# Attention row sums spread by VectorE and DMA instead of TensorE, longer PV runs, one PV bank for two query groups

## The reference, cut to what matters

```python
mod = (_silu(L0_c) @ L0_wmod).reshape(1, 6, 1, -1)           # sa, ca, ga, sb, cb, gb
h = _layernorm(x) * (1 + ca) + sa
qkv = jnp.einsum('bse,ehd->bshd', h, w_qkv)                  # E=128, H=16, 3*64
q, k, v = jnp.split(qkv, 3, axis=-1)
logits = where(tril, einsum('bqhd,bkhd->bhqk', q, k) / sqrt(64), very_low)
att = einsum('bhqk,bkhd->bqhd', softmax(logits), v)
x = x + ga * einsum('bshd,hde->bse', att, w_out)             # ga, gb kept off zero
h = _layernorm(x) * (1 + cb) + sb
expert = argmax(h @ Wr.T + br)                               # 8 experts
y = W2[expert] @ relu(W1[expert] @ h + b1[expert]) + b2[expert]   # 128 -> 512 -> 128
x = x + gb * y
```

## Time and profile before

| | |
|---|---|
| time, median of 3 | 1067.04 us (1066.79 to 1068.41) |
| profiled execution, its own time | 1067.29 us |
| its span, first to last instruction | 1065.5 us |
| mean granted clock of TensorE | 0.98 |
| TensorE busy | 999.7 us (94%) |
| ScalarE busy | 718.6 us (67%) |
| VectorE busy | 701.0 us (66%) |
| attention's steady part | 38 to 948 us |
| routing and scatter | 948 to 1000 us |
| 23 expert tiles | 1000 to 1064 us |

### The profile page before, as it was taken

How to read it: one execution, slowest core, us unless ns; L and a number is a source line. 1 busy time by engine, 2 the same in 40 slices (tenths; PEclk the granted TensorE clock), 3 DMA queues, 4 the chain that set the end, 5 groups by cost and what they waited for, 6 DMA issues and landing times.

```text
span 1065.5 us, 19784 instructions
## 1 busy us (share of the span) xinstructions
PE 999.7 (94%) x7275; PEld 762.3 (72%) x7275; DVE 701.0 (66%) x2234; ACT 718.6 (67%) x1317; POOL 43.1 (4%) x55
## 2 busy tenths in 40 slices
PE   4999999999999999999999999999999999986386
PEld 2677777777777777777777777777777777755376
DVE  4976667856866577666785686657766678555264
ACT  2977767767667677776776776767777677642264
POOL 0000000000000000000000000000000000002444
PEclk9999999999999999999999999999999999996699
DMA  9300020002100020002000210002000100030210
GB/s 202 70 21 1 22 50 21 2 10 48 34 1 2 20 51 21 1 21 50 22 1 19 47 26 1 2 20 51 21 2 21 41 21 1 2 99 16 59 50 17
DMA packets 33199, 31.53 MB, mean 30 GB/s; under 512 B 12181, under 2 KB 22209, under 8 KB 33104
## 3 DMA queue, kind: packets, MB, share of 16 engines
q1 hardware_dynamic: 31856, 28.15, 11.3%
q0 software_dynamic: 1248, 2.13, 0.6%
HBM read 9.83 MB, written 4.12 MB: 13 GB/s over the span
## 4 chain that ended last, share of the span: by engine, by line
PE 85%; DVE 5%; issue 3%; POOL 2%; ACT 1%; DMA 1%; DVEq 1%; SPq 0%; POOLq 0%
PE ps L619 25%; PE ps L656 24%; PE ps L630 22%; PE ps L598 5%; PE ps L639 3%; PE ps L667 3%; PE ps L602 2%; POOL x_sorted L557 1%; DVEq L1067 1%; DVE q_split L926 1%; ACT q_split L791 1%; PE ps L707 1%; PE ps L733 1%; DVE accT L1086 1%; DVE v_sb L1100 1%
## 5 line engine op out<-in xcount | busy, mean ns | idle before, releaser
L619 PE MATMUL ps<-k_split,q_split 128*128 128x512 f32 (+2 forms) x1280 | 370.1, 396 | 4.1 <-DVE q_split L926 2.0
L805 ACT ACTIVATE probs<-probs,neg_max 128x128 f32<-128x128 f32 (+15 forms) x256 | 308.5, 1206 | 41.7 <-DVE neg_max L954 39.4
L947 DVE TENSOR_SCALAR_CACHE_REDUCE probs<-ps 128x512 f32<-128x512 f32 (+1 forms) x384 | 249.6, 667 | 100.0 <-PE ps L630 66.7
L813 ACT COPY pT<-ps 128x512 f32<-128x512 f32 (+1 forms) x435 | 234.2, 564 | 109.7 <-PE ps L630 105.6
L630 PE MATMUL ps<-ident,probs 128*128 128x128 f32 x2176 | 304.4, 273 | 1.4 <-DVE pT L966 1.3
L630 PEld LDWEIGHTS ps<-ident,probs 128*128 128x128 f32 x2176 | 256.0, 140 | 60.7 <-issue 29.4
L656 PE MATMUL ps<-pT,v_sb 128*64 128x256 f32 (+1 forms) x2304 | 272.6, 373 | 0.0
L619 PEld LDWEIGHTS ps<-k_split,q_split 128*128 128x128 f32 x1280 | 201.0, 190 | 48.8 <-issue 28.6
L656 PEld LDWEIGHTS ps<-pT,v_sb 128*64 128x64 f32 x2304 | 152.3, 136 | 87.1 <-issue 26.6
L950 DVE CUSTOM_DVE_ANT_0 probs<-ps,causal 128x256 f32<-128x256 f32 (+3 forms) x256 | 130.9, 511 | 27.6 <-PE ps L619 26.3
L966 DVE COPY pT<-ps 128x512 f32<-128x512 f32 (+1 forms) x141 | 92.3, 659 | 32.9 <-PE ps L630 30.2
(11 more groups left out here) (126 smaller groups left out, 610.4 us busy)
## 6 DMA issues: line engine op xcount, KB each, us to landing
k_split<-k_split SPq DMA_DIRECT2D x64, 256.0 KB, 3.7
probs<-in_L_ffn_W_dram SPq DMA_DIRECT2D x1, 2048.0 KB, 8.5
w_pair<-in_L_attn_w_qkv_dram SPq DMA_DIRECT2D x24, 64.0 KB, 3.1
hT<-x_sorted SPq DMA_DIRECT2D x23, 65.5 KB, 1.9
x_sorted<-zeros SPq DMA_DIRECT2D x1, 1495.0 KB, 13.8
x_sb<-in_L_attn_x_dram SPq DMA_DIRECT2D x4, 256.0 KB, 5.3
wo_pair<-in_L_attn_w_out_dram SPq DMA_DIRECT2D x8, 64.0 KB, 2.6
probs<-in_L_ffn_b_dram SPq DMA_DIRECT2D x1, 512.0 KB, 9.7
```

The source lines that it names most:

```text
L619: m = pe.matmul(ps_ring[:, s.bank, 0:w], q_split[r % 2][:, q0:q0 + P], k_split[r % 2][:, part, k0:k0 + w], start=(part == 0), stop=(part = ...
L805: act.activation(row, row, ACT.Exp, bias=neg_max[:, g, r:r + 1], accum_out=row_sum[:, g, r:r + 1]).then_inc(exp_done, 1)
L813: act.copy(pT[:, n % PT_SLOTS, lo:BANK], ps_turn[:, n % TURN_BANKS, lo:BANK]).then_inc(turn_taken[n % TURN_BANKS], 1)
L947: dve.tensor_scalar(row, ps_ring[:, bank, 0:w], 1.0, LOWEST, ALU.mult, ALU.max, accum_out=highest).then_inc(bank_free[bank], 1)
```

## The change

Six edits, made together:
1. The reciprocals no longer go through TensorE and ScalarE. VectorE writes them into a 128x32 tile and turns it in 32x32 blocks; SyncE stores 4 rows of each block to DRAM (put, 4 DMAs) and loads them back broadcast over 64 partitions (get, 2 DMAs), 64 groups in all. bcast and spread are gone.
2. ps_o holds two groups, each in its half; norm works on 512 columns once per two groups, and pv waits for it at even groups only.
3. PV_BATCH goes from 6 to 11 and the clause on a whole group goes; SCORE_TILES, PROJ_LEAD, BIAS are changed in the planner.
4. SyncE's order comes from the plan (keys, put, get, weights, by planned time).
5. ones and earlier lie in pT and are made by GpSimd after the last pv; zeros is a part of causal.
6. In the expert loop the value_load is ahead of the wait for y_full instead of behind the add.

```diff
-PV_BATCH = 6
+PV_BATCH = 11
 SCORE_LEAD = 1.4
-PROJ_LEAD = 2
+SCORE_TILES = 20.0
+TAKE_ACT = -400.0
+TAKE_DVE = 0.0
+ADD_DVE = 0.0
+PROJ_LEAD = 1
+PUT = 3600.0
+GET = 4800.0
+PUTS = 4
+SQUARE = 32
-    BIAS = dict(act=dict(take=-800.0), dve=dict(take=300.0, add=2000.0))
+    BIAS = dict(act=dict(take=TAKE_ACT), dve=dict(take=TAKE_DVE, add=ADD_DVE))
...
         if kind == "pv":
-            past = group_before(p, g) if key[2] == 0 else None
-            return max(at("take", *key), at("value", p, key[2] // 4), at("norm", *past) if past else 0.0)
+            past = group_before(p, g) if key[2] == 0 and g % 2 == 0 else None
+            return max(at("take", *key), at("value", p, key[2] // 4), at("norm", past[0], past[1] // 2) if past else 0.0)
         if kind == "norm":
-            return max(at("spread", p, g), at("pv", p, g, 2 * g + 1), at("out", p - 1, g // 2) if p else 0.0)
+            return max(self.got(p, 2 * g), self.got(p, 2 * g + 1), at("pv", p, 2 * g + 1, 4 * g + 3),
+                       at("out", p - 1, g) if p else 0.0)
+    def get_from(self, p, g):
+        before = p * CHUNKS + g // 2 - 2
+        free = self.at("norm", before // CHUNKS, before % CHUNKS) if before >= 0 else 0.0
+        return max(self.at("sum", p, g) + PUT, free)
+    def got(self, p, g):
+        return self.get_from(p, g) + GET
+    def transfers(self):
+        steps = []
+        for p in range(PAIRS):
+            for c in range(CHUNKS):
+                steps.append((self.at("lo", p, c, 1), "keys", (p, c)))
+            for g in range(GROUPS):
+                steps.append((self.at("sum", p, g), "put", (p, g)))
+                steps.append((self.get_from(p, g), "get", (p, g)))
...
-        in_pv = self.mode in ("pv", "bcast")
-        pv_past = not self.ahead["pv"] or (self.ahead["bcast"] and self.ahead["pv"][0][:2] > self.ahead["bcast"][0])
-        order = [("bcast", in_pv or pv_past), ("pv", in_pv), ("proj", due <= PROJ_LEAD),
-                 ("pv", waiting >= PV_BATCH or (whole and waiting >= min(PV_BATCH, 3))),
-                 ("out", True), ("back", True), ("score", score_at - turn_at < SCORE_LEAD), ("turn", True),
-                 ("score", True), ("pv", True), ("proj", due <= PROJ_LEAD + 2), ("bcast", True)]
+        early = score_at - turn_at < SCORE_LEAD and self.tiles_to(score_at) - self.tiles_to(turn_at) < SCORE_TILES
+        order = [("pv", self.mode == "pv"), ("proj", due <= PROJ_LEAD), ("pv", waiting >= PV_BATCH),
+                 ("out", True), ("back", True), ("score", early), ("turn", True), ("score", True), ("pv", True),
+                 ("proj", due <= PROJ_LEAD + 2)]
...
+                elif s.kind == "put":
+                    sp.wait_ge(rinv_ready, n + 1)
+                    for a in range(P // SQUARE):
+                        sp.dma_start(spread_rows[n, :, a * SQUARE:(a + 1) * SQUARE],
+                                     rinv_rows[a * SQUARE:a * SQUARE + 4, n % PUTS, :]
+                                     ).then_inc(spread_put[n % PUTS], 16)
+                elif s.kind == "get":
+                    n, part = p * GROUPS + g, p * NC + g // 2
+                    sp.wait_ge(spread_put[n % PUTS], 64 * (n // PUTS) + 64)
+                    if part >= 2:
+                        sp.wait_ge(o_ready, part - 1)
+                    for h in range(2):
+                        sp.dma_start(rinv_b[own_half(h), part % 2, QG * (g % 2):QG * (g % 2) + QG
+                                            ].rearrange("p (u i) -> p u i", u=2),
+                                     spread_rows[n:n + 1, h::2, :].broadcast_to([D, 2, P])
+                                     ).then_inc(spread_in[part % 2], 16)
...
+            pool.wait_ge(pv_done, plan.total["pv"])
+            nc.gpsimd.memset(ones, 1.0).then_inc(sort_made, 1)
...
                 elif s.kind == "pv":
-                    if j == 0 and p + g:
-                        pe.wait_ge(o_ready, p * GROUPS + g)
+                    if j == 0 and g % 2 == 0 and p + g:
+                        pe.wait_ge(o_ready, p * NC + g // 2)
...
-                    dve.reciprocal(rinv[:, g, :], row_sum[:, g, :]).then_inc(rinv_ready, 1)
+                    n = p * GROUPS + g
+                    if n >= PUTS:
+                        dve.wait_ge(spread_put[n % PUTS], 64 * (n // PUTS))
+                    dve.reciprocal(rinv[:, n % PUTS, 0:4], row_sum[:, g, :]).then_inc(rinv_made, 1)
+                    dve.wait_ge(rinv_made, n + 1)
+                    dve.transpose(rinv_rows[:, n % PUTS, :], rinv[:, n % PUTS, :]).then_inc(rinv_ready, 1)
...
-                    b_bank, b_use = plan.bank_of("bcast", p, g)
-                    dve.wait_ge(bank_free[b_bank], b_use + 1)
+                    dve.wait_ge(spread_in[part % 2], 64 * (part // 2) + 64)
-                    dve.tensor_tensor(oT[:, g * QG:(g + 1) * QG], ps_o[:, 0:QG], rinv_b[:, g % 2, :],
+                    dve.tensor_tensor(oT[:, c * BANK:(c + 1) * BANK], ps_o[:], rinv_b[:, part % 2, :],
                                       ALU.mult).then_inc(o_ready, 1)
...
+                following = expert_of(k + CHOSEN) if k + CHOSEN < SLOTS else None
                 dve.wait_ge(y_full, k + 1)
...
                     dve.wait_ge(y_taken, k + 1)
-                    copy_expert(k + CHOSEN, k % CHOSEN)
+                    copy_expert(following, k % CHOSEN)
```

More of the change, by code:

```diff
@@ L65 @@
 class Plan:
-    IN_RING = ("score", "bcast", "out", "proj", "back")
-    EMPTIES = {"top": "score", "lo": "proj", "value": "proj", "spread": "bcast", "add": "out", "resid": "back"}
+    IN_RING = ("score", "out", "proj", "back")
+    EMPTIES = {"top": "score", "lo": "proj", "value": "proj", "add": "out", "resid": "back"}
     def __init__(self):
@@ L80, in __init__ @@
         ends = [(PAIRS - 1, c) for c in range(CHUNKS)]
-        keys = dict(score=scores, turn=turns, pv=turns, bcast=groups, out=parts,
+        keys = dict(score=scores, turn=turns, pv=turns, out=parts,
                     proj=[(p, c, j) for p, c in parts for j in range(3)], back=ends,
                     top=scores, exp=[(p, g, r) for p, g in groups for r in range(4)], take=turns,
-                    hi=splits, lo=splits, value=parts, sum=groups, spread=groups, norm=groups,
+                    hi=splits, lo=splits, value=parts, sum=groups, norm=parts,
                     add=parts, resid=ends)
@@ L110, in __init__ @@
         self.span = max(clock.values())
+        self.sp = self.transfers()
         self.ring_uses = [len(range(b, len(self.uses), RING)) for b in range(RING)]
-    KINDS = dict(pe=("score", "turn", "pv", "bcast", "out", "proj", "back"),
-                 act=("spread", "hi", "value", "take", "exp"),
+    KINDS = dict(pe=("score", "turn", "pv", "out", "proj", "back"),
+                 act=("hi", "value", "take", "exp"),
                  dve=("norm", "sum", "lo", "add", "resid", "top", "take"))
-    FIRST = dict(act=("spread", "hi", "value"), dve=("sum", "norm", "lo"))
-    BIAS = dict(act=dict(take=-800.0), dve=dict(take=300.0, add=2000.0))
+    FIRST = dict(act=("hi", "value"), dve=("sum", "norm", "lo"))
+    BIAS = dict(act=dict(take=TAKE_ACT), dve=dict(take=TAKE_DVE, add=ADD_DVE))
     def at(self, kind, *key):
@@ L170, in ready @@
         return at({"hi": "proj", "lo": "hi", "add": "out", "resid": "back"}[kind], *key)
+    def get_from(self, p, g):
[12 more added lines that the diff above has]
+                steps.append((self.get_from(p, g), "get", (p, g)))
+            if p + 1 < PAIRS:
+                steps.append((self.at("lo", p, 1, 1) + HOP, "qkv_weights", (p + 1,)))
+                steps.append((max(self.at("lo", p, 2, 1), self.at("out", p - 1, CHUNKS - 1) if p else 0.0) + HOP,
+                              "out_weights", (p + 1,)))
+        order = [Step(kind, key, 0, 0) for _, kind, key in sorted(steps)]
+        begun = [0, 0]
+        for s in order:
+            if s.kind in ("put", "get"):
+                begun[s.kind == "get"] += 1
+                assert begun[0] - begun[1] <= PUTS
+        return order
     def bank_of(self, kind, *key):
@@ L179, in took @@
         if engine == "pe":
-            columns = self.mode in ("pv", "bcast")
-            if kind == "bcast":
-                return 440.0 + (0.0 if columns else 142.0)
+            columns = self.mode == "pv"
             if kind == "pv":
@@ L236, in choose_pe @@
         turn_at = place("turn", lambda k: k[2] / float(tiles_of(k[1])))
-        waiting, whole = 0, False
+        waiting = 0
         for key in self.ahead["pv"]:
@@ L408, in adaln_block @@
         negmax_ready = sem("negmax_ready")
+        rinv_set = sem("rinv_set")
+        rinv_made = sem("rinv_made")
         rinv_ready = sem("rinv_ready")
+        spread_put = [sem(f"spread_put{i}") for i in range(PUTS)]
+        spread_in = [sem(f"spread_in{i}") for i in range(2)]
         exp_done = sem("exp_done")
@@ L486, in _ @@
```

(6 more changed lines are left out.)

131 lines of the change are left out of this document (69 added, 62 removed).

## The result

The changed kernel takes 1015.41 us (median of 4 runs, 1014.45 to 1016.63) against 1067.47 us for the kernel before on the same chip. The ratio is 0.9512, with a 95% interval of 0.9496 to 0.9529: 52 us off. Forecast were 42 us off, 1024.7 us, with a range of 1012 to 1045. The profiled execution took 1014.77 us, its span is 1012.7 us.

The account below looks back on a forecast made before the run. TensorE was taken to bound attention, VectorE and its sequencer the expert loop. 28.2 + 12.1 + 8.8 - 6.4 - 0.3 = 42.4 us off the profiled 1067.3 us gave 1024.9, put at 1024.7 us for the median; range 1012 to 1045.

Parts of the forecast that it names:

- Part 1: Attention: bcast and spread leave TensorE, 28.2 us off; VectorE's added turn is covered, the DMA chain taken as 7 us.
- Part 2: Attention, one PV bank for two groups: waits at 8 starts of a pair lose 6.4 us (bounds 0 and 25).
- Part 3: Attention, longer runs of PV: 39 runs fewer at 0.31 us each, 12.1 us off (bounds 7.1 and 17.1).
- Part 4: End of attention: the last norm adds 0.3 us; the matrices GpSimd makes before the sort cost zero.
- Part 5: Expert loop: the early load of the expert number shrinks VectorE's gap, 8.8 us off (bounds 0 and 9.7).
- (d): Rival, attention: norm waits for rows from DRAM at all 32 boundaries, 83 us lost, 1102 us, slower than before; chance 0.04.
- (a): Rival, attention: longer PV runs and later projections leave VectorE, ScalarE or keys late, 22 us of stall, 1040 us; chance 0.15.
- (b): Rival, attention: PV runs don't get longer, cut by even groups' waits and 12 slots, 1037 us; chance 0.07.
- (c): Rival, expert loop: the load isn't hidden, since the sequencer doesn't pass the add of x, 1033.5 us; chance 0.08.

Follow-up runs that it names:

- e2: The changed kernel with the four small matmuls of a bcast put back ahead of each group's first PV: 1040.74 us, ratio 0.9759 to the kernel before.
- e3: The kernel before with only the expert number loaded ahead of the wait for y_full: 1057.25 us, ratio 0.9904.
- e7: The changed kernel with the first of the two key-doubling DMAs sent after the first subtraction instead of after both: 1005.27 us, ratio 0.9418.
- e8: The changed kernel with the planner's price for doubled keys at 4600 ns instead of 3600, and SCORE_TILES 26 instead of 20: 1007.35 us, ratio 0.9424.
- e5: The kernel before with PV_BATCH 11 instead of 6 and without the clause on a whole group: 1073.05 us, ratio 1.0058.
- e1: The changed kernel with PV_BATCH 6 in place of 11, all else kept: 1014.33 us, ratio 0.9502 to the kernel before.
- e6: The kernel before with all planner constants and rules of the changed one, but bcast, spread and norm per group kept: 1067.66 us, ratio 0.9995.
- e9: e7 with PV_BATCH 6 in place of 11, 100 runs of PV against 71: 1012.29 us, ratio 0.9488 to the kernel before.
- e10: The changed kernel with three more DMAs in each group's chain, each waited for by SyncE, order of steps unchanged: 1041.70 us, ratio 0.9774.

## Why the prediction was right, and where it was off

**What bounds the kernel.** Right in both halves: columns taken from TensorE came off in attention (e2), and in the expert loop the sequencer of VectorE was the bound (e3). That the work added to VectorE and taken from ScalarE counts for nothing fits the traces, in which TensorE waits for neither in the steady part, but no run changed that work alone.

**Part 1.** 28.2 us forecast; 27.6 by e2. The price read inside a run (0.44) was the right row, not the 273 ns x 4 of the groups. Turn: 0.2 forecast, 0.212 measured. The DMA chain: 7 us forecast, 5.4 measured, just under my lower bound of 5.7. The two parts erred in opposite ways: put took 2.1 us where the bound had 3.2 (it was through 0.9 us after its four issues, where I had 1.8), and get 3.2 us where the bound had 2.5 (its landing takes 2.6 us, not 1.8).

**Part 2.** 6.4 us of new stall forecast; the waits rose by 4.6 us (4.1 to 8.7). The size was near, the mechanism half right: not one wait of TensorE was for a norm. All were for doubled keys, which I had named as the second thing due at the same places. e7 and e8 show that these waits go when the keys come sooner or are priced higher, 3.6 us being too low: after the changed kernel's first subtractions of the trace, SyncE issues at 33.98 and the keys land at 38.65, 4.7 us.
```profile
33.98 0.59 SPq L541
34.57 0.04 issue
34.62 4.03 DMA k_split<-k_split
```
The price alone doesn't bring the waits, though: the kernel before has the same 3.6 us and 0.8 us of waits for keys, e5 (longer runs alone) has 1.2, e1 (short runs in the changed kernel) 0.5, and e6 (all the constants on the kernel before) 7.7. They come when long runs and the other constants, PROJ_LEAD 1 among them, meet the low price.

**Part 3.** This is the term that was mis-sized. I took 103 idle records before PV's weight loads for 103 runs. The order of steps has 128; the changed one has 71 where I had 64 (its trace shows 59 such records). So 57 runs went, not 39. At the 0.31 us of the chain that is 17.7 us, at e9's 0.24 us 13.7, where 12.1 were forecast. The price of a run was right: TensorE's busy time gives 0.32 us in e1, 0.27 in e5, 0.28 from e7 to e9. What e1 and e5 teach is that this saving can't be added alone: the waits took it back in e1 and took more than it in e5, where the same rule lost 5 us.

**Part 4.** Last norm 0.70 for 0.43 us, nothing from the sort's matrices: routing stayed at 52 us.

**Part 5.** 8.8 us forecast, 10.4 by e3, 10.7 by the windows. I had capped the gain by the 9.7 us of idle weight loads and left 0.05 us per tile of them; in fact the tiles run at 1.89 us, and once the stage has begun 0.4 us of such idle time is left in it. The Trainium skill's 600 ns for such a load (DMA: Bandwidth & Descriptors, "Latency and other measured facts") fits only the slowest of the 23 loads of the kernel before, 0.62 us; their median is 0.30 us. The changed kernel's take 0.30 to 0.56 us, median 0.37. By the estimate that hung on the 600 ns the gain would have been 5 us less, and it wasn't.

**The sum again, with what was measured.** 27.6 (bcast) + 17.7 or 13.7 (runs) - 4.6 (keys) + 10.4 (early load) = 51.1 or 47.1 us, of 52.1. By busy time the steady part closes so: 46.4 us less, of which 27.5 are bcast's, leaves 18.9 us for 57 runs, 0.33 us each, a little above the 0.27 to 0.32 of the other pairs; so up to 5 us may be something else that no run isolates. Forecast were 42.4. The 9.7 us between are mostly 5.6 us of runs that I had miscounted (by the chain's price), some 2 us less stall, and 1.6 us in the expert loop. That the miscount fell on the safe side is luck.

**The rivals.** A slip in (d): 28.2 + 12.1 + 8.8 - 0.3 is 48.8, so I took the 0.3 off twice; the time would be 1101, not 1102. (a), stall in place of gain, is what e5 shows on the kernel before, not on the changed one. (b) fell with the runs of 12 tiles. (c) fell with e3. (d) was built in e10: a chain 2.6 us over the plan cost 26 us, not 83, since it became a wait at a few places and not at all 32 boundaries; the change still gains there. Where it did, TensorE lost the wait in full, as (d) has it, and its lower clock after it besides. The Trainium skill's warning on DMA's fixed cost (DMA: Bandwidth & Descriptors, "Anatomy of one DMA") stands as a figure, though it is given for GpSimd's path and these transfers go from SyncE: one leg through DRAM took 1.87 us here, near its 2.0. Put, whose target is DRAM too, was through 0.9 us after its issues. Both were hidden.

## What to carry to other kernels

When an engine is full for the whole of a stage, price an edit by the pitch in the chain inside a run of equal instructions, and look for small matmuls that only move data: a detour of 2 KB through DRAM, 5.4 us long, was free here, because the result was wanted later than that. Count runs in the program's order, not by idle records in a trace. And do not credit an order rule by itself: longer runs were worth -5 us (e5), 0 (e1) and +7 us (e9 to e7) on three kernels, according to which wait came next, so look at the waits after each change and then take away the new one, here by an earlier transfer (e7, 10 us) or by the planner's price for it (e8, 8 us).

## What the runs showed that I had not expected

- A sequencer's register load ran under VectorE's own work: moved ahead of a wait, it took 0.61 us of a 0.76 us gap with it.
- A DMA queue's waits are paid by its other customers: in e10 one TensorE wait for keys was 8.4 us long, behind transfers of 2 KB.
- A wait costs TensorE more than its length: in e10 its granted clock was at 0.50 for about 3 us or more after each of two waits of over 8 us, and its busy time rose by 7 us.
- Sending one of two 256 KB transfers 0.69 us sooner (e7) took nearly all 8.7 us of nine waits, more than the 9 x 0.69 = 6.2 us of the earlier start. The transfers also landed sooner after their issue: the longest took 4.6 us in place of 5.4, and the one behind the changed kernel's wait of 1.76 us took 5.00 us there and 3.98 us in e7. That issuing the two back to back slows them is my guess; no run tests it.
